# A fused attention and FP4 feed-forward block on one core: the same work with a new order for every batch, split first steps, and exp(q) kept in SBUF

## The reference

```python
xn  = _layernorm(x, axis=-1)
x   = x + attn(xn) + ffn(xn)

def attn(x):                                  # 16 heads of 8, code size 2
    q, k, v = split(x @ w_qkv.T)              # by heads
    q = einsum('bhtd,hcd->bhtc', q, code) * scale
    k = einsum('bhtd,hcd->bhtc', k, code) * scale
    q = softmax(q, axis=-1) * scale
    k_exp = exp(k - max(k, axis=2, keepdims=True))
    k_exp_cumsum = cumsum(k_exp, axis=2)      # along the positions
    kv = cumsum(einsum('bhtc,bhtd->bhtcd', k_exp, v), axis=2) / (k_exp_cumsum[..., None] + 1e-09)
    return merge(einsum('bhtc,bhtcd->bhtd', q, kv)) @ w_out.T

def ffn(x):                                   # 128 -> 352 -> 128
    gate, y = fp4_linear(x, w_gate), fp4_linear(x, w_up)
    return fp4_linear(silu(gate) * y, w_down)
# fp4_linear rounds both its operands to FP4 in blocks of 16 (scale = max|block| / 6), dequantizes, multiplies
```

## Time and profile before

| | |
|---|---|
| median of 3 runs | 136.61 us (136.31 to 136.81) |
| span of the profiled execution, first to last instruction | 134.5 us |
| from that span to the median | 2.1 us |
| PE busy | 125.9 us (94%) |
| DVE busy | 121.8 us (91%) |
| POOL busy | 116.5 us (87%) |
| ACT busy | 114.0 us (85%) |
| TensorE clock granted | 1.00 of full speed |

### The profile page before, as it was taken

One profiled execution on the slowest core, in us unless ns is written; L12 is line 12 of the kernel. 1 busy time (PEld: TensorE's weight loads), 2 busy tenths in 40 slices (PEclk: granted clock), 3 DMA queues, 4 the chain that ended last, 5 costly groups with the idle time before them and its releaser, 6 DMA issues.

```text
span 134.5 us, 2464 instructions
## 1 busy us (share of the span) xinstructions
PE 125.9 (94%) x821; PEld 106.4 (79%) x821; DVE 121.8 (91%) x293; ACT 114.0 (85%) x280; POOL 116.5 (87%) x118
## 2 busy tenths in 40 slices
PE   2999999795999999999999999999999998999992
PEld 2999977564577878887898798879887986889892
DVE  2789999898999899989998999899999997999971
ACT  0498997989999998999999999999998788698540
POOL 5387887899989999999999999999999999998600
DMA  4992000000000001000010002000200020010022
GB/s 110 276 389 88 5 2 0 2 0 2 0 0 5 0 0 77 1 0 5 35 43 0 2 5 80 0 0 0 78 5 0 0 78 0 0 58 25 0 97 59
DMA packets 4363, 5.14 MB, mean 38 GB/s; under 512 B 576, under 2 KB 2432, under 8 KB 4352
## 3 DMA queue, kind: packets, MB, share of 16 engines
q1 hardware_dynamic: 3264, 4.44, 9.5%
q10 hardware_dynamic: 1088, 0.56, 1.4%
HBM read 2.90 MB, written 2.10 MB: 37 GB/s over the span
## 4 chain that ended last, share of the span: by engine, by line
PE 78%; ACT 10%; DVE 4%; POOL 4%; issue 2%; POOLq 0%
PE at_ps L1910 5%; PE o_ps L2131 3%; PE o_ps L2115 3%; PE o_ps L1951 3%; PE o_ps L1842 2%; PE u_ps L2136 2%; ACT xn L653 2%; PE u_ps L1877 2%; PE u_ps L2021 2%; PE h_ps L2056 2%; PE h_ps L1901 2%; PE g_ps L2032 2%; PE g_ps L1890 2%; PE at_ps L1696 2%; PE at_ps L1719 2%; PE at_ps L1720 2%
## 5 line engine op out<-in xcount | busy, mean ns | idle before, releaser
L453 POOL TENSOR_TENSOR kv<-v_sb,kv 128x1024 f32<-128x1024 f32 x6 | 11.8, 1972 | 0.0
L361 POOL TENSOR_TENSOR o_codes<-kv,q_n 128x1024 f32<-128x1024 f32 x6 | 11.8, 1967 | 0.0
L1910 PEld LDWEIGHTS at_ps<-wqkv_t,xn_t 128*128 128x128 f32 x48 | 8.0, 190 | 3.2 <-DVE q_n L1285 2.2
L1910 PE MATMUL at_ps<-wqkv_t,xn_t 128*128 128x192 f32 x48 | 8.9, 328 | 1.6 <-DVE q_n L1285 1.6
L653 ACT ACTIVATE xn<-x_all,shift,rstd 128x128 f32<-128x128 f32 x24 | 9.8, 483 | 0.0
L402 POOL TENSOR_TENSOR yh<-h,h_r 128x704 f32<-128x704 f32 x6 | 8.3, 1388 | 1.2 <-ACT h_r L735 1.2
L344 POOL TENSOR_TENSOR hq<-qh,h_max 128x704 f32<-128x704 bf16 x6 | 8.3, 1385 | 0.1
L419 POOL TENSOR_TENSOR hq<-qh,h_max 128x704 f32<-128x704 bf16 x6 | 8.3, 1388 | 0.0
L483 POOL TENSOR_TENSOR yh<-h,h_r 128x704 f32<-128x704 f32 x6 | 8.3, 1391 | 0.0
L1099 DVE TENSOR_TENSOR kv<-kv,at_ps 128x1152 f32<-128x1152 f32 x6 | 8.0, 1337 | 0.0
L1044 ACT ACT_TABLE_LOAD x6 | 7.7, 1283 | 0.1
(11 more groups left out here) (497 smaller groups left out, 512.8 us busy)
## 6 DMA issues: line engine op xcount, KB each, us to landing
x_all<-x SPq DMA_DIRECT2D x8, 256.0 KB, 4.8
out<-out_sb SPq DMA_DIRECT2D x7, 256.0 KB, 2.0
out<-out_sb SPq DMA_DIRECT2D x4, 64.0 KB, 1.6
w_raw<-w_down ACTq DMA_DIRECT2D x1, 176.0 KB, 4.7
w_raw<-w_up ACTq DMA_DIRECT2D x1, 128.0 KB, 3.2
w_raw<-w_gate SPq DMA_DIRECT2D x1, 128.0 KB, 3.2
wqk_raw<-w_qkv ACTq DMA_DIRECT2D x1, 128.0 KB, 4.7
wqkv_t<-w_qkv ACTq DMA_DIRECT2D x1, 64.0 KB, 4.4
```

The source lines that it names most:

```text
L361: nc.gpsimd.tensor_tensor(o_codes[:, p, :, :].rearrange("p j (c w) -> p j c w", w=HEAD), kv[:, p, :, 0:KV].rearrange("p j (c w) -> p j c w ...
L453: nc.gpsimd.tensor_tensor(kv[:, p, :, 0:KV].rearrange("p j (c h w) -> p j c h w", c=CODE, w=HEAD), v_sb[:, p, :].rearrange("p (j h w) -> p ...
L1910: last = nc.tensor.matmul(at_ps[:, j // 2, j % 2 * QKV:(j % 2 + 1) * QKV], xn_t[:, p, j * P:(j + 1) * P], wqkv_t[:, :], start=(j % 2 == 0) ...
```

## The change

The program is written anew with one function per operation and an explicit list of calls for each engine. What it computes is the same.

- Every batch now has an order of its own, on every engine, and each call is told its PSUM bank: `ps` is one tensor of 8 banks, and a bank may serve any purpose.
- The gate and the up weights are rounded by separate chains (384 columns each, formerly one of 768); of batch 0, x is rounded in halves of two tiles.
- For batch 0 and batch 7 scaling and dequantization of h go by single tile on POOL. The four dequantizations of batch 7, formerly on DVE, are on POOL.
- The small steps of the layer norm (`var_eps`, `ratio`, `rstd`, `shift`) move from ACT and POOL to DVE; only the first root is still on POOL (`root(0, 1)`).
- exp(-q) (`q_exp`), its sum (`q_sum`) and exp(-log den) (`den_exp`) are SBUF tensors.
- PE has 13 blocks of unread products instead of 20, all ahead of the first weights.

```diff
-                    nc.scalar.activation(a_ps[:, ROW:ROW + TILES * HC].rearrange("p (j c) -> p j c", j=TILES), q_rel[:, p, :, :], ACT.Exp, scale=-1.0).then_inc(qexp_done, 1)
+            def q_exp_of(b):
+                return nc.scalar.activation(q_exp[:, b % 2, :, :], q_rel[:, b % 2, :, :], ACT.Exp, scale=-1.0)
...
-                    nc.vector.tensor_tensor(den_p[:, :, :].rearrange("p j c -> p (j c)"), a_ps[:, 0:TILES * HC], den[:, :, :].rearrange("p j c -> p (j c)"), ALU.mult).then_inc(dprod_done, 1)
+            def den_check(b):
+                p = b % 2
+                return nc.vector.tensor_tensor(den_p[:, p, :, :], den_exp[:, p, :, :], den[:, p, :, :], ALU.mult)
...
+            def denominators(b):
+                p = b % 2
+                for c in range(CODE):
+                    last = nc.vector.scalar_tensor_tensor(out=den[:, p, :, c * HEADS:(c + 1) * HEADS], in0=kv[:, p, :, KV + c * HEADS:KV + (c + 1) * HEADS],
+                                                          scalar=DEN_EPS, in1=q_sum[:, p, :, :], op0=ALU.add, op1=ALU.mult)
+                return last
...
+            def den_newton(b):
+                p = b % 2
+                return nc.vector.scalar_tensor_tensor(out=den_r[:, p, :, :], in0=den_p[:, p, :, :], scalar=2.0, in1=den_exp[:, p, :, :], op0=ALU.subtract, op1=ALU.mult)
...
+            def q_normal(b):
+                p = b % 2
+                return nc.vector.scalar_tensor_tensor(out=q_n[:, p, :, :], in0=q_exp[:, p, :, :], scalar=-HEAD_SCALE, in1=den_r[:, p, :, :], op0=ALU.mult, op1=ALU.mult)
...
+            pool.wait_ge(kexp_done, 1)
+            k_times_v(0).then_inc(kvm_done, 1)
...
+            h_dequant(7, 3, 4).then_inc(hq_done, 1)
```

More of the change, by code:

```diff
@@ L314, in _ @@
+            sp.dma_start(w_raw[0:FF - 2 * P, 2 * P:FFP], w_gate[2 * P:FF, :]).then_inc(gate_in, 16)
             sp.dma_start(x_all[:, 1, :], x_v[1]).then_inc(x_in[1], 16)
             sp.wait_ge(x_in[0], 16)
[L317 to L329, removed]
+            sp.dma_start(x_all[:, 2, :], x_v[2]).then_inc(x_in[2], 16)
+            sp.dma_start(wo_t[:, :], w_out_t).then_inc(wo_in, 16)
@@ new lines, in unread, with qk_weights, w_transpose @@
+            def unread():
+                for _ in range(2):
+                    nc.tensor.matmul(ps[:, 7, 0:P], ident[:, :], before[:, :], start=True, stop=True)
+            def qk_weights(bank):
+                for s in range(2):
+                    last = nc.tensor.matmul(ps[:, bank, s * HC:(s + 1) * HC], wqk_raw[:, s, :], code_bd[:, s, :, :].rearrange("p c h -> p (c h)"), start=True, stop=True)
+                return last
+            def w_transpose(w, bank):
+                first = {"gate": 0, "up": FFP, "down": 2 * FFP}[w]
+                for c in range(CHUNKS):
+                    last = nc.tensor.transpose(ps[:, bank, c * P:(c + 1) * P], w_dq[:, first + c * P:first + (c + 1) * P], ident[:, :])
+                return last
@@ new lines, in prefix, with transpose_o @@
+            def prefix(b, bank):
+                return nc.tensor.matmul(ps[:, bank, 0:ROW], before[:, :], kv[:, b % 2, TILES - 1, :], start=True, stop=True)
+            def transpose_o(b, bank):
+                p = b % 2
+                for j in range(TILES):
+                    nc.tensor.matmul(ps[:, bank, j * P:(j + 1) * P], o_codes[:, p, j, 0:D], ident[:, :], is_transpose=True, start=True, stop=False)
+                    last = nc.tensor.matmul(ps[:, bank, j * P:(j + 1) * P], o_codes[:, p, j, D:KV], ident[:, :], is_transpose=True, start=False, stop=True)
+                return last
@@ new lines, in transpose_hq, with project @@
+            def transpose_hq(b, j, bank):
+                for c in range(CHUNKS):
+                    last = nc.tensor.transpose(ps[:, bank, c * P:(c + 1) * P], hq[:, b % 2, j, c * P:(c + 1) * P], ident[:, :])
+                return last
+            def project(b, bank, start):
+                for j in range(TILES):
+                    last = nc.tensor.matmul(ps[:, bank, j * P:(j + 1) * P], o_t[:, b % 2, j * P:(j + 1) * P], wo_t[:, :], start=(start and j == 0), stop=False, skip_group_check=True)
+                return last
```

3939 lines of the change are left out of this document (1970 added, 1969 removed).

## The result

The changed kernel takes 156.84 us (median of 4 runs, 154.68 to 158.08) against 136.53 us before (4 runs by now): a ratio of 1.1356 with a 95% interval of 1.1279 to 1.1433. The forecast was 135.0, with a range of 133 to 148. The profiled execution took 154.68 us, with a span of 152.6, so that 2.1 us lie around it, as before.

What follows compares the result with a forecast made beforehand. PE and POOL were taken as both full in batches 1 to 6, with gains only at the ends. POOL's stream, 17.3 + 108.2 + 2.5 + 4.9 = 132.9 us of span, plus 2.1 around it, gave 135.0 us, range 133.0 to 148.0.

Steps and rivals of the forecast that it cites:

- The second rival: DVE's two-SBUF-input instructions stand behind POOL's, on the chain from prefix to o_codes; 148 us (142 to 155), chance 0.31.
- the lower bound: Five DVE instructions per batch with two SBUF inputs cost nothing, if DVE and POOL read without regard for each other.
- the upper bound: Each of five DVE instructions per batch waits until POOL's current instruction ends: 0.67 us on average, 3.3 us per batch.
- the sum by POOL's stream: Span from POOL's first kv start, its work, idle time and the end: 17.3 + 108.2 + 2.5 + 4.9 = 132.9 us.
- the idle time: POOL's waits after its first kv product: taken as 2.5 us, between 0 and the 4.3 of before.
- the start: POOL's first kv product, waiting for exp(k) on ACT, starts near 17.3 us, against 17.76 before.
- of work: POOL's own instructions from its first kv product on: 108.2 us, against 104.5 before.
- behind POOL's end: Transpositions, copy, down products, residual, hops and store after POOL's last instruction: 4.9 us, against 8.0 before.
- The full price: Waits of DVE's five two-SBUF-input instructions: 2.9 us for each of seven batches, about 20 us, then taken at two thirds, 13.
- Edits at nothing: Edits costed at nothing, among them some 13 layer norm steps moved to DVE, near 2 us, within DVE's over 10 us room.
- The first: Start's gain is given back in batches 2 to 6: 136.8 us at 4.3 us POOL idle, 138.5 at 6; chance 0.20.
- The third: At the start exp(k) comes at 18 or later and PE starves until 23: 136 us, inside the forecast's 0.49 chance.

Runs made afterwards that it cites:

- the run with exp(-q) alone: The kernel before with only exp(-q) moved to SBUF, so only q_n has two SBUF inputs: 138.95 us, ratio 1.0164.
- the 40 free of waiting: Changed kernel, the 40 DVE instructions of the denominators and normalised q replaced by one-element maxima, layer norm's 13 kept: 139.18 us, ratio 1.0219.
- the two reduce runs: Changed kernel with two-SBUF-input DVE instructions replaced by one-element tensor_reduce maxima: all 53, 136.55 us; only the 40 of denominators and normalised q, 139.18 us.
- the reduce run: Changed kernel with all 53 two-SBUF-input DVE instructions replaced by a one-element tensor_reduce maximum, var_eps unchanged: 136.55 us, ratio 0.9989.
- the last reduce run: Changed kernel with all 53 two-SBUF-input DVE instructions and also var_eps as one-element maxima: 134.99 us, ratio 0.9858.
- the run with silu times silu: The kernel before with h made as silu times silu, so 32 longer DVE instructions have two SBUF inputs: 154.0 us, a single run.

## Why the prediction was wrong

**The choice between the bounds failed.** The second rival had the mechanism, and the changed kernel's trace shows it: `den` in the place named, over 0.5 us, its end at the end of POOL's instruction. I gave it 0.31 and took the lower bound as the forecast, "because these are the shortest instructions of DVE and because DVE's room would cover up to about 1.2 us for each batch". Both reasons fall. The length doesn't matter, since the wait is for what is left of POOL's instruction (`ratio`, 8 columns: 1.92 us). And DVE has little room in the middle: in the run with exp(-q) alone, one wait of 0.45 us (`q_n` at 59.21 with 741 ns for 291) moved its period from 13.77 to 69.78 - 55.78 = 14.00 us, so about 0.2 us were free, not 1.2. The summed 10 us over the span lay at the ends: from 40 to 110 us DVE idled 2.5 us in all. The prediction disagreed with itself here, since its second rival gives DVE 13.4 us of work in 13.8. The rule of the Trainium skill named there spoke for the upper bound, and the runs bear it out.

In the terms of the sum by POOL's stream, the term that failed is the idle time. The sum was 17.3 + 108.2 + 2.5 + 4.9 = 132.9 us of span; the changed kernel has 16.2 for the start, 110.0 of work, 21.1 of idle time and 5.3 behind POOL's end, 152.6. POOL's idle time was taken at 2.5 us, and it is 21.1, because DVE's instructions stand behind POOL's, and what POOL needs from DVE then comes late: its waits for `qh`, `q_n` and `qx` are 8.6, 5.5 and 4.5 us.

**The price was then cut by a third, wrongly.** The full price was put at 3.3 us for a batch and 20 us in all, and cut to 13 because a late DVE leaves POOL idle more often. On DVE the five cost (14.8 + 5.2 + 4.1 + 3.0 - 9.3) / 8 = 2.2 us for a batch, with 9.3 for the same 40 in the form that doesn't wait; less than 3.3, since `q_n` was mostly spared (377 ns on average, with a median of 284). But nearly all of it reached the time: with the 40 free of waiting, the kernel was 155.3 - 139.2 = 16.1 us faster, which is 2.0 for each of the 8 batches. The upper end of the range, 148, rested on the cut value; the full price of 20 us gives the 155 that the rival names for the case that all five wait, which is where the kernel stands, though 16.1 us of it come from the five and the rest from the next point.

**Edits at nothing.** The 13 steps of the layer norm, "near 2 us" and hidden, cost 2.6 us by the two reduce runs. In the changed kernel's trace five of them are longer than in the reduce run, by 4.0 us together, all of it in the first 50 us, where they stand ahead of `q_n` and of the k maximum for which PE waits. They too have two SBUF inputs; I had looked for these only on the chain of the denominators. `var_eps` has the other form that waits, but in the changed kernel it didn't have to wait (158 to 170 ns); its 1.6 us (136.55 - 134.99) belong to the reduce run alone.

**Right, once the waits are taken out.** The profiled execution of the last reduce run has the span of the sum, 132.9 us: `kv` starts at 16.77, POOL waits 2.1 us in all, its last instruction ends at 127.5, 5.4 us ahead of the end, and 108.6 us are left for the work. The time is 134.99 where 135.0 was forecast. Each term is within 0.6 us, and that the errors cancel so exactly is luck; the runs lie between 133.8 and 136.3. So in this run the new orders are worth 1.4%, the batch-7 dequantizations and single tiles included. That run leaves out part of the arithmetic, though at the same count and shape of instructions; no complete version showed the gain. (For the kernel before, the prediction had 104.5 us of work and 4.3 of idle time; the idle times that its trace gives add up to 3.8, which leaves 105.0 of work. The forecast used this only as a bound of its own idle time.)

**The first and third rivals** did not come about: in the last reduce run POOL waits no more than 0.4 us at a time behind 32 us. The third had exp(k) late and PE starved until 23 us. exp(k) was early, but PE did starve, to 1.39 of 5 us busy ahead of 20 us and a clock of 0.50 behind it, and in the last reduce run to 2.23 and 0.66; the prediction had the first gate product near 22 us (it came at 24.3, and at 22.7 in the last reduce run) but no price for a lower clock.

## What to carry to other kernels

Where POOL is nearly always at work, look at every DVE instruction for how many SBUF inputs it has: one operand in PSUM, or the form `tensor_reduce`, kept the short ones at 0.2 to 0.3 us here, a `reciprocal` kept its own time, and two SBUF inputs, or `tensor_scalar` from SBUF to SBUF, cost the rest of POOL's instruction. Two such instructions back to back cost most, and short ones cost as much as long ones. A tensor that sits in PSUM "only" because there was room may be what keeps two engines apart; and an experiment that replaces an instruction must show by its durations that the replacement is free of what it is to exclude.

## What the runs showed of the hardware

- A wait of DVE for POOL is part of the instruction's own duration, up to 2.0 us for 64 columns (`den`, 215 to 2005 ns), and in one case lasted over two of POOL's instructions: `var_eps` in the first reduce run started in the first (1.05 us) and ended 0.04 us behind the second (0.78 us).
- `tensor_scalar` with one SBUF input waits like an instruction with two (729 ns on average for `den`, where two inputs had 962), and the one-element maximum in the same place does not (208 ns).
- POOL is held up as well, by 0.27 to 0.28 us behind a DVE instruction that takes 0.5 us alone: `hq` 1.66 us for 1.39, a `kv` addition 1.08 for 0.80 (the run with silu times silu).
- A reciprocal of 128 columns takes 942 ns on average in the old order and 946 in the new one, and each of the 16 lies between 936 and 955 ns.
